# Expert stage of a transformer block: low halves made by GpSimd subtractions instead of by matmuls with minus one

## What is computed

```python
def _L0_ffn_ref(x, Wr, Wg, Wu, Wd):
    probs = jax.nn.softmax(x @ Wr, axis=-1)
    topk_w, topk_idx = jax.lax.top_k(probs, 2)
    topk_w = topk_w / jnp.sum(topk_w, axis=-1, keepdims=True)
    output = jnp.zeros_like(x)
    for i in range(8):
        sel = topk_idx == i
        w_i = jnp.sum(topk_w * sel, axis=-1, keepdims=True)
        h = jax.nn.silu(x @ Wg[i]) * (x @ Wu[i])     # 512 -> 512
        output = output + w_i * (h @ Wd[i])          # 512 -> 512
    return output
```

## Time and profile before

| | |
|---|---|
| median of 3 runs | 1139.51 us (1138.58 to 1140.64) |
| the profiled execution | 1142.83 us |
| its span, first to last instruction | 1140.9 us |
| mean granted TensorE clock in it | 0.978 |
| TensorE busy, share of the span | 1087.6 us, 95% |
| VectorE busy | 774.6 us, 68% |
| ScalarE busy | 697.5 us, 61% |
| GpSimd busy | 522.7 us, 46% |
| first gate product of the experts' stage | 918.09 us |

### The profile page before, as it was taken

How to read it: one execution, slowest core, us unless ns; L and a number is a source line. 1 busy time by engine, 2 the same in 40 slices (tenths; PEclk the granted TensorE clock), 3 DMA queues, 4 the chain that set the end, 5 groups by cost and what they waited for, 6 DMA issues and landing times. The chain is left out here.

```text
span 1140.9 us, 19556 instructions
## 1 busy us (share of the span) xinstructions
PE 1087.6 (95%) x5681; PEld 897.2 (79%) x5681; DVE 774.6 (68%) x1561; ACT 697.5 (61%) x2031; POOL 522.7 (46%) x601
## 2 busy tenths in 40 slices
PE   4599999999999999999999999998999789999996
PEld 3488888888888888888888888886888667877885
DVE  7999986977776896777697766667454874655000
ACT  7668788767788857888876567763241324434432
POOL 6755664455444454455445544442000325555432
PEclk8899999999999999999999999999999889999999
DMA  7221111151111115111114111103943347573310
GB/s 267 105 77 56 37 45 36 37 208 46 37 44 54 46 36 192 54 36 45 37 36 163 45 36 44 54 19 110 341 163 141 130 163 219 178 238 94 54 44 0
DMA packets 52819, 107.39 MB, mean 94 GB/s; under 512 B 6064, under 2 KB 27056, under 8 KB 51184
## 3 DMA queue, kind: packets, MB, share of 16 engines
q1 hardware_dynamic: 48016, 97.00, 25.8%
q0 software_dynamic: 4704, 9.18, 3.5%
HBM read 91.48 MB, written 16.52 MB: 95 GB/s over the span
## 5 line engine op out<-in xcount | busy, mean ns | idle before, releaser
L523 POOL TENSOR_TENSOR rs<-va,mhalf 125x2 f32<-125x2 f32 (+1 forms) x180 | 202.4, 1125 | 14.1
L545 POOL TENSOR_TENSOR c_lo<-c_raw,c_hi 128x500 fp32r<-128x500 f32 x96 | 124.3, 1295 | 184.4 <-ACT c_hi L604 162.7
L516 POOL TENSOR_TENSOR va<-ss,epst 125x2 f32<-125x2 f32 (+1 forms) x180 | 57.5, 319 | 159.9 <-DVE ss L1103 99.9
L818 PE MATMUL bank<-w_hi,c_hi 128*125 128x512 f32 x384 | 120.1, 435 | 6.7 <-ACT w_hi L599 6.2
L791 PE MATMUL bank<-w_hi,xqs 128*128 128x512 f32 (+2 forms) x464 | 110.0, 359 | 10.7 <-DVE xqs L1095 10.7
L818 PE MATMUL bank<-w_lo,c_hi 128*125 128x512 f32 x384 | 105.8, 397 | 0.0
L818 PE MATMUL bank<-w_hi,c_lo 128*125 128x512 f32 x384 | 105.4, 396 | 0.0
L687 ACT ACTIVATE work<-bank,nmax 112x375 f32<-112x375 f32 x128 | 73.6, 587 | 44.3 <-DVE nmax L1132 44.0
L791 PE MATMUL bank<-w_lo,xqs 128*128 128x512 f32 (+2 forms) x464 | 100.4, 338 | 0.1
L862 PE MATMUL bank<-kxT,qxT 128*112 128x375 f32 x256 | 96.9, 480 | 0.0
L818 PEld LDWEIGHTS bank<-w_hi,c_hi 128*125 128x125 f32 x384 | 67.2, 188 | 25.0 <-issue 6.4
(11 more groups left out here) (277 smaller groups left out, 2823.4 us busy)
## 6 DMA issues: line engine op xcount, KB each, us to landing
c_raw<-in_ctxT SPq DMA_DIRECT2D x96, 250.0 KB, 2.6
shared<-in_w_in SPq DMA_DIRECT2D x13, 1024.0 KB, 8.3
shared<-in_wproj SPq DMA_DIRECT2D x32, 256.0 KB, 4.2
raw_g<-in_Wg SPq DMA_DIRECT2D x8, 1024.0 KB
raw_u<-in_Wu SPq DMA_DIRECT2D x8, 1024.0 KB, 5.9
raw_d<-in_Wd SPq DMA_DIRECT2D x8, 1024.0 KB, 5.6
cat_scratch<-results SPq DMA_DIRECT2D x32, 224.0 KB, 2.0
shared<-cat_scratch SPq DMA_DIRECT2D x2, 1792.0 KB, 9.1
```

The source lines that it names most:

```text
L516: pool.tensor_tensor(va[0:rows, lo:hi], ss[0:rows, lo:hi], epst[0:rows, lo:hi], ALU.add).then_inc(va_done, 1)
L523: pool.tensor_tensor(rs[0:rows, lo:hi], va[0:rows, lo:hi], mhalf[0:rows, lo:hi], ALU.pow).then_inc(rs_done, 1)
L545: pool.tensor_tensor(flat(c_lo[:, k, :, :]), flat(c_raw[:, k, :, :]), flat(c_hi[:, k, :, :]).bitcast(F32), ALU.subtract).then_inc(cl_done, 1)
L818: m = pe.matmul(bank[0:CT, :], a[:, ch, k, :], w[:, k, CKX:CV], start=(i == 0), stop=(i == 3 * KB - 1))
```

## The change

The matmuls with minus one (`rest_of_rows`, `rest_of_inner`) are removed. ScalarE evicts from the bank of transposes the high half and then the same values whole: the rows back over `xr` (`rows_whole`), the inner value back over `hf` (`inner_high_and_whole`). GpSimd subtracts: `rows_low` computes xl = xr - xh, `inner_low` computes hl = hf - hh, each 128x512 (the last inner value in two halves). GpSimd's list for tile i is now product(i), low rows(i+1), add(i-1), low inner(i), gather(i+3); the add of tile i-1 in the last round moves behind the low inner halves. `products` takes the eight products with high halves first and then waits for the low half before the last four; before, the three kinds alternated and the low half was waited for ahead of all. The down products are no longer interrupted; the register load stands between gate and up products.

```diff
@@ gpsimd
         def gather(i):
             if i >= 3:
-                pool.wait_ge(tx_rdy, i - 2)
+                pool.wait_ge(xl_done, i - 2)
...
             if i >= 1:
-                pool.wait_ge(th_rdy, i)
+                pool.wait_ge(hl_done, i)
             pool.tensor_tensor(hf[:, :], sg[:, :], up_out[:, :], ALU.mult).then_inc(hf_done, 1)
+
+        def rows_low(i):
+            pool.wait_ge(xh_done, i + 1)
+            pool.wait_ge(xw_done, i + 1)
+            if i >= 2:
+                pool.wait_ge(u_rdy, i - 1)
+            pool.tensor_tensor(xl[:, i % 2, :], xr[:, i % 3, :], xh[:, i % 2, :].bitcast(F32),
+                               ALU.subtract).then_inc(xl_done, 1)
+
+        def inner_low(i):
+            for n, (_, cols) in enumerate(inner_banks(i)):
+                pool.wait_ge(hh_done, i + 1 + n)
+                pool.wait_ge(hw_done, i + 1 + n)
+                if i >= 1:
+                    pool.wait_ge(dn_rdy, i)
+                pool.tensor_tensor(hl[:, cols], hf[:, cols], hh[:, cols].bitcast(F32),
+                                   ALU.subtract).then_inc(hl_done, 1)
...
         for i in range(TI):
             product(i)
-            if i >= 1:
+            if i + 1 < TI:
+                rows_low(i + 1)
+            if 1 <= i < TI - 1:
                 add(i - 1)
+            inner_low(i)
             if i + 3 < TI:
                 gather(i + 3)
+        add(TI - 2)
         add(TI - 1)
@@ scalar
-        def rows_low(i):
-            act.wait_ge(sx_rdy, i + 1)
-            act.activation(xl[:, i % 2, :], p_x[:, :], ACT.Copy).then_inc(xl_done, 1)
+        def rows_whole(i):
+            act.activation(xr[:, i % 3, :], p_x[:, :], ACT.Copy).then_inc(xw_done, 1)
...
             for bank, cols in inner_banks(i):
                 act.activation(hh[:, cols], bank[:, cols], ACT.Copy).then_inc(hh_done, 1)
+                act.activation(hf[:, cols], bank[:, cols], ACT.Copy).then_inc(hw_done, 1)
...
         for i in range(TI):
             gated(i)
-            if i >= 1:
-                inner_low(i - 1)
             upward(i)
             if i + 1 < TI:
                 rows_high(i + 1)
-                rows_low(i + 1)
+                rows_whole(i + 1)
             if 1 <= i < TI - 1:
                 result(i - 1)
-            inner_high(i)
-        inner_low(TI - 1)
+            inner_high_and_whole(i)
@@ tensor
-        def products(bank, a_hi, a_lo, n, at, ks):
-            for k in ks:
-                for m in range(3):
-                    a, w = ((a_hi, hi), (a_hi, lo), (a_lo, hi))[m]
+        def products(bank, a_hi, a_lo, low, n, at):
+            for m, (a, w) in enumerate(((a_hi, hi), (a_hi, lo), (a_lo, hi))):
+                for k in range(KB):
+                    if m == 2 and k * len(low) % KB == 0:
+                        pe.wait_ge(*low[k * len(low) // KB])
...
         for i in range(TI):
-            pe.wait_ge(xl_done, i + 1)
+            pe.wait_ge(xh_done, i + 1)
...
+            if i + 1 < TI:
+                at[i + 1], split[i + 1] = weights_of(i + 1)
             if i >= 1:
-                rest_of_inner(i - 1)
                 pe.wait_ge(up_done, i)
...
             if i >= 1:
-                pe.wait_ge(hl_done, i)
+                pe.wait_ge(hh_done, i)
                 if i >= 2:
                     pe.wait_ge(y_done, i - 1)
-                products(pd, hh[:, :], hl[:, :], 2, at[i - 1], (0, 1))
-            if i + 1 < TI:
-                rest_of_rows(i + 1)
-                at[i + 1], split[i + 1] = weights_of(i + 1)
-            if i >= 1:
-                products(pd, hh[:, :], hl[:, :], 2, at.pop(i - 1), (2, 3)).then_inc(dn_rdy, 1)
+                products(pd, hh[:, :], hl[:, :], ((hl_done, i),), 2, at.pop(i - 1)).then_inc(dn_rdy, 1)
             turn_inner(i)
```

More of the change, by code:

```diff
@@ L1431, in projected_experts @@
     xh_done = sem(c, "xh_done")
-    sx_rdy = sem(c, "sx_rdy2")
+    xw_done = sem(c, "xw_done")
     xl_done = sem(c, "xl_done")
@@ L1440, in projected_experts @@
     hh_done = sem(c, "hh_done")
-    sh_rdy = sem(c, "sh_rdy")
+    hw_done = sem(c, "hw_done")
     hl_done = sem(c, "hl_done")
@@ L1561, in _ @@
             gather(i)
+        rows_low(0)
         pool.wait_ge(row_done, 2)
@@ L1630, in upward, with inner_high_and_whole @@
             act.activation(up_out[:, :], pu[:, :], ACT.Copy).then_inc(up_done, 1)
-        def inner_high(i):
+        def inner_high_and_whole(i):
             act.wait_ge(th_rdy, i + 1)
@@ L1637, in inner_high @@
                 act.activation(hh[:, cols], bank[:, cols], ACT.Copy).then_inc(hh_done, 1)
-        def inner_low(i):
-            for n, (bank, cols) in enumerate(inner_banks(i)):
-                act.wait_ge(sh_rdy, i + 1 + n)
-                if i >= 1:
-                    act.wait_ge(dn_rdy, i)
-                act.activation(hl[:, cols], bank[:, cols], ACT.Copy).then_inc(hl_done, 1)
+                act.activation(hf[:, cols], bank[:, cols], ACT.Copy).then_inc(hw_done, 1)
         def result(i):
@@ L1654, in _ @@
         rows_high(0)
-        rows_low(0)
+        rows_whole(0)
         for i in range(TI):
             gated(i)
-            if i >= 1:
-                inner_low(i - 1)
             upward(i)
@@ L1769, in turn_rows @@
             if i >= 1:
-                pe.wait_ge(xl_done, i)
+                pe.wait_ge(xw_done, i)
             for k in range(KB):
-                mm = pe.matmul(p_x[:, k * P:(k + 1) * P], xr[:, i % 3, k * P:(k + 1) * P], ident[:, :],
-                               start=(k == 0), stop=False, is_transpose=True, skip_group_check=True)
+                mm = pe.transpose(p_x[:, k * P:(k + 1) * P], xr[:, i % 3, k * P:(k + 1) * P], ident[:, :])
             mm.then_inc(tx_rdy, 1)
[L1776 to L1779, removed]
         def turn_inner(i):
@@ L1783, in turn_inner @@
             if i >= 1:
-                pe.wait_ge(hl_done, i)
+                pe.wait_ge(hw_done, i)
+            if i == TI - 1:
+                pe.wait_ge(xw_done, TI)
             banks = inner_banks(i)
@@ L1787, in turn_inner @@
                 bank = banks[k * len(banks) // FB][0]
-                mm = pe.matmul(bank[:, k * P:(k + 1) * P], hf[:, k * P:(k + 1) * P], ident[:, :],
-                               start=(k * len(banks) % FB == 0), stop=False, is_transpose=True,
-                               skip_group_check=True)
+                mm = pe.transpose(bank[:, k * P:(k + 1) * P], hf[:, k * P:(k + 1) * P], ident[:, :])
             mm.then_inc(th_rdy, 1)
[L1793 to L1797, removed]
-        def products(bank, a_hi, a_lo, n, at, ks):
-            for k in ks:
-                for m in range(3):
-                    a, w = ((a_hi, hi), (a_hi, lo), (a_lo, hi))[m]
+        def products(bank, a_hi, a_lo, low, n, at):
[3 more added lines that the diff above has]
+                        pe.wait_ge(*low[k * len(low) // KB])
                     mm = pe.matmul(bank[:, :], a[:, k * P:(k + 1) * P],
@@ L1824, in _ @@
                 pe.wait_ge(sg_done, i)
-            products(pg, xh[:, i % 2, :], xl[:, i % 2, :], 0, at[i], range(KB)).then_inc(g_rdy, 1)
+            rows = xh[:, i % 2, :], xl[:, i % 2, :], ((xl_done, i + 1),)
+            products(pg, *rows, 0, at[i]).then_inc(g_rdy, 1)
             if i == 0:
                 gates_to_rows()
+            if i + 1 < TI:
+                at[i + 1], split[i + 1] = weights_of(i + 1)
             if i >= 1:
-                rest_of_inner(i - 1)
                 pe.wait_ge(up_done, i)
             pe.wait_ge(l_done[1], split[i])
-            products(pu, xh[:, i % 2, :], xl[:, i % 2, :], 1, at[i], range(KB)).then_inc(u_rdy, 1)
+            products(pu, *rows, 1, at[i]).then_inc(u_rdy, 1)
             pe.wait_ge(l_done[2], split.pop(i))
@@ L1836, in _ @@
             if i >= 1:
-                pe.wait_ge(hl_done, i)
+                pe.wait_ge(hh_done, i)
                 if i >= 2:
                     pe.wait_ge(y_done, i - 1)
-                products(pd, hh[:, :], hl[:, :], 2, at[i - 1], (0, 1))
-            if i + 1 < TI:
-                rest_of_rows(i + 1)
-                at[i + 1], split[i + 1] = weights_of(i + 1)
-            if i >= 1:
-                products(pd, hh[:, :], hl[:, :], 2, at.pop(i - 1), (2, 3)).then_inc(dn_rdy, 1)
-            turn_inner(i)
[L1847 to L1851, removed]
+                products(pd, hh[:, :], hl[:, :], ((hl_done, i),), 2, at.pop(i - 1)).then_inc(dn_rdy, 1)
+            turn_inner(i)
+        pe.wait_ge(hh_done, TI + 1)
+        products(pg, hh[:, :], hl[:, :], ((hl_done, TI), (hl_done, TI + 1)), 2, at[TI - 1]).then_inc(dn_rdy, 1)
     @block.vector
```

1 line of the change is left out of this document (removed).

## The result

The changed kernel takes 1141.99 us, the kernel before 1140.39 (medians of 20 runs each): a ratio of 1.0015, 95% interval 1.0009 to 1.0021. It is slower by 1.6 us, where I had forecast 16 more. The profiled execution of the changed kernel is the shortest of its 20 (1139.69 us, span 1138.0), and the one of before would be among the longest of its own (1142.83, span 1140.9). So the two spans must not be set against each other; distances within a tile can.

A forecast was written before the change was run, and what follows sets the result against it. TensorE was taken to pace the experts' stage. Minus products -9.3, head -1.3, burst stops +19.2 and clock +8.0 sum to +16.6: 1159.4 us from the profiled execution, 1156 beside the median; range 1136 to 1164.

The forecast's parts named there:

- Minus products, -9.3: TensorE, tiles 1 to 20: removing 40 products with minus one at 0.233 us each saves 9.3 us.
- The head, -1.3: Tile 0: TensorE goes straight on to its gate products with high halves, starting them 1.3 us sooner.
- Add as now, 1.37 to 4.93: GpSimd in a burst: add held by `lo_d`, 1.37 to 4.93 us from the first gate product, unchanged.
- third rival: Burst: the add isn't held by `lo_d`, product 0.55 us late; -8.9 us in all, 1131; chance 0.05.
- Low inner asks at 4.95, is held to 6.9: Burst: GpSimd's inner low half waits for `lo_g`, runs to 8.2, pushes the cast of `hi_u` behind it; 0.25 us lost.
- Gather ends 10.3, product held to 11.7, ends 13.0: Burst: gather held to 9.4, product held by `lo_u`; TensorE 3.85 us later per burst than now, +19.2 for five.
- second rival: Burst: low inner slips in ahead of `lo_g`, product ends at 10.8, 1.65 us later than now; 1137 to 1145; chance 0.18.
- Clock, +8.0: TensorE's clock falls to 0.50 after each of five burst stops, 1.6 us each; bounds 0 and +15.
- Bursts before 950, counted at nothing: Weight splits before 950 us, at the stage's start, cost nothing; a hold or two of 1.3 us within range.
- a chain of four holds: Burst: add, low inner, gather and product on GpSimd each held by VectorE; a stop of some 4 us; chance 0.65.
- one tie of 0.3 us: Burst: low inner asks at 4.95, `lo_g` started at 4.65; claimed `lo_g` goes first, all later holds hanging on it.

The follow-up runs named there:

- without VectorE: VectorE's weight splitting for experts 2 to 7 left out of both kernels: changed 1127.95 us, before 1139.82 us.
- the run with the shortest cast: Changed kernel with the cast `hi_g` of experts 2 to 7 over only 512 of 2048 columns: 1141.31 us (1.0007).
- the run with the gather ahead: Changed kernel with gather(i+3) moved ahead of add(i-1) and low inner(i) in GpSimd's list: 1150.8 us (1.0091).
- quarters: Changed kernel with VectorE's weight subtractions of experts 1 to 7 in four instructions of 512 columns: 1128.92 us (0.9902).

## Why the prediction was wrong, step by step

- *Minus products, -9.3.* Right: 9.27 per tile, where 9.78 less the two products is 9.31. The 0.04 beyond them go with the order of the products, which alone gave 0.08. 20 x 0.51 = 10.2 and the head's 1.2 make 11.4; the change is worth 11.9 us without VectorE. I had -10.6.
- *The head, -1.3.* Right: the gate products of tile 0 start 1.57 behind the first transposes of the rows (913.97 to 915.54), where before it was 2.73 (915.36 to 918.09): 1.2 us.
- *Add as now, 1.37 to 4.93.* Right: 3.57, held by `lo_d`. The third rival is out.
- *"Low inner asks at 4.95, is held to 6.9."* **This is the step that failed.** I took the recorded end of the add for the time at which GpSimd's next instruction asks, and the recorded start of `lo_g` for the moment at which VectorE owns the port. In the trace the low half starts 4.7 behind the gate products' start (972.83 less 968.09) and goes first, taking 1.51 and not 3.25; in the run with the shortest cast it goes first even with `lo_g` recorded 0.58 ahead.
- *Gather ends 10.3, product held to 11.7, ends 13.0.* Both follow from that step and fall with it. The gather was held longer than I had it (3.25, not 1.8), the product not at all: it ends at 979.05, 11.0 behind the gate products' start at 968.09. That is the second rival, "one hold fewer", which had 10.8. Per burst it had 1.65 of stop more than today; measured are some 2.1, and 1.0 net of the two tiles' gain.
- *Clock, +8.0.* Mis-sized: one stretch in one trace and two in the other, 1.5 us each, instead of five. The stops were 2 us and not 4, and even then only 5 of 20 had one.
- *Bursts before 950, counted at nothing.* Nearly right. 3.1 of the 14 us that TensorE waits for the product lie there, 2.3 of them in tile 0; the other two places are 0.6 and 0.2. Tile 0's stop is hardly a new one: before, TensorE waits 0.74 there, does the minus product of the rows in 0.50, and waits 0.76 for the product, 2.0 together, and now the same time is one stop. What I left out is its clock: in 8 of the 11 traces with the rows' part of the change there is a stretch at 0.50 close behind this stop, and in 1 of the 5 without. From the transposes of tile 1's rows to those of tile 3's it is then 19.4 to 20.9 us instead of 18.2 to 19.1. What of it is in the timed runs is in the 11.9 already.
- *The sum as it is:* -11.9 without VectorE; five stops of 2.0 to 2.6 us, 10.9 together where today it is 0.1 each, so +10.4; +1.5 to 3 for the clock; +0.8 in tiles 1 and 2: +0.8 to +2.3. Measured +1.6, inside the second rival's range. The direction and the mechanism, the port that VectorE and GpSimd share, were right; without it the change gains 1%. The size was off by a factor of ten, since a small result is left when two terms of 10 to 14 us nearly cancel, and an error in one of them is then an error of the whole.
- *Chance.* I gave 0.65 to a chain of four holds that all hung on one tie of 0.3 us, and 0.18 to the case that came.

The Trainium skill (SBUF — State Buffer, section Who interferes with whom) says that whoever issues first keeps the pair for its whole instruction. The product held by `lo_u` in the run with the gather ahead agrees. Two things don't follow from it: `lo_g` is recorded 0.58 us ahead of the low half and yet runs behind it, and a gather recorded 1.9 us ahead of the cast of `hi_u` (974.51 and 976.43) is held to that cast's end. Either the recorded start isn't the moment of issue, or the rule doesn't hold beside an indirect DMA; no run here tells which.

## What to carry to other kernels

Before work moves to GpSimd, look at what VectorE runs at that hour: not the sum of GpSimd's busy time decides, but which of its instructions is held, and whether a deadline lies behind it. Where the other engine has slack, cut its long two-input instructions into pieces: halves of 1024 columns turned a loss of 0.15% into a gain of 1%. No finer than needed: quarters bring nothing more and leave the other engine almost no pause. And where two large terms oppose each other, the range has to reach to their difference with either one at its other bound.

## What the hardware showed that I had not expected

- GpSimd's instruction behind an indirect DMA is recorded as starting before the DMA's own end: 0.2 to 0.5 us (972.83 against 973.02; 974.12 against 974.57).
- An indirect gather of 1.0 us takes 2.95 to 3.25 when it meets a subtraction and then a cast on VectorE; it ends 0.1 behind the cast. In quarters it takes 1.3 to 1.8.
- A VectorE subtraction of 2.29 us took up to 4.77, with two GpSimd instructions of 1.28 inside it, and TensorE waited for none of it.
- A stop of TensorE of 2 us brought its clock to 0.50 in 5 of 20 cases (four traces); a pair of such stops 1.3 us apart had it down for 7 us, three times of three.
- VectorE's six instructions of a burst, 11.8 us before, took 19.6 once the subtractions were in quarters with GpSimd's work in between (967.48 to 987.05).
